# A product-based recommender network on one NeuronCore: all whole row chunks moved by SyncE through a DRAM passage

## What is computed

```python
embed = tables[jnp.arange(26)[None, :], sparse_inputs]      # 2048 x 26 x 32, float32
p   = jnp.einsum('bfe,bge->bfg', embed, embed)
l_z = jnp.einsum('bfe,feh->bh', embed, w_z)                 # h = 256
l_p = jnp.einsum('bfg,fgh->bh', p, w_p)
l_1 = relu(concatenate([l_z + l_p + l_b, dense_inputs], axis=-1))   # dense: 13
h   = relu(l_1 @ W1 + b1)                                   # 128
out = sigmoid(h @ Wf + bf)                                  # 2048 x 1
```

## Time and profile before

| | |
|---|---|
| time, median of 3 runs | 599.81 us (599.52 to 599.99) |
| span of the profiled execution, first to last instruction | 548.8 us |
| POOL busy | 409.0 us (75%), 430 instructions |
| DVE busy | 417.5 us (76%), 250 instructions |
| ACT busy | 139.7 us (25%), 333 instructions |
| PE busy | 131.1 us (24%), 204 passes |
| mean granted TensorE clock | 0.683 of full speed |
| DMA: indirect gathers | 13312 packets, 6.84 MB |
| DMA: issued by SyncE | 6318 packets, 2.63 MB |

### The profile page before, as it was taken

How to read it: one execution, slowest core, us unless ns; L and a number is a source line. 1 busy time by engine, 2 the same in 40 slices (tenths; PEclk the granted TensorE clock), 3 DMA queues, 4 the chain that set the end, 5 groups by cost and what they waited for, 6 DMA issues and landing times.

```text
span 548.8 us, 1701 instructions
## 1 busy us (share of the span) xinstructions
PE 131.1 (24%) x204; PEld 48.0 (9%) x204; DVE 417.5 (76%) x250; ACT 139.7 (25%) x333; POOL 409.0 (75%) x430
## 2 busy tenths in 40 slices
PE   0000000415334100060465100051433600005067
PEld 0000000201111000020121000020110100002023
DVE  4204199998992369998996419999899547999995
ACT  0000004404551021704452010340455110250323
POOL 6777777777777777777777777777777777777792
PEclk9999999976567555585666655567665555558569
DMA  6222323122122222222112222222112222312220
GB/s 148 21 14 13 13 13 14 13 13 14 14 13 13 13 13 14 13 14 13 13 14 14 13 13 13 13 14 13 14 13 13 14 14 13 14 13 13 13 46 2
DMA packets 19640, 9.56 MB, mean 17 GB/s; under 512 B 9888, under 2 KB 19629, under 8 KB 19629
## 3 DMA queue, kind: packets, MB, share of 16 engines
q0 software_dynamic: 13312, 6.84, 22.4%
q1 hardware_dynamic: 6318, 2.63, 2.1%
HBM read 8.85 MB, written 0.01 MB: 16 GB/s over the span
## 4 chain that ended last, share of the span: by engine, by line
POOL 69%; issue 23%; DVE 6%; DMA 1%; PE 1%; ACT 0%; ACTq 0%; POOLq 0%; DVEq 0%
POOL rows L286 66%; DVE pairs L368 3%; DVE prod L348 2%; POOL prod L302 2%; POOL prod L313 1%; DMA rows<-in_L_rec_tables,which 1%; PE ps_h L643 0%; DMA raw<-in_r_sparse_inputs 0%; DVE pair_rows L404 0%; PE ps_h L680 0%; ACT scores L551 0%; PE ps_copy L692 0%; ACT hidden L537 0%; ACTq L120 0%; DVE pairs_T L395 0%
## 5 line engine op out<-in xcount | busy, mean ns | idle before, releaser
L286 POOL DMA_INDIRECT rows<-in_L_rec_tables,which x416 | 393.5, 946 | 128.4 <-issue 125.8
L348 DVE TENSOR_TENSOR prod<-ps_copy,rows 128x1664 f32<-128x1664 f32 (+12 forms) x103 | 194.2, 1910 | 16.8 <-ACT ps_copy L471 16.8
L368 DVE TENSOR_REDUCE pairs<-prod 128x76 f32<-128x2432 f32 (+13 forms) x73 | 195.3, 2680 | 0.0
L626 PE MATMUL ps_h<-field_rows,wz 128*128 128x512 f32 x96 | 59.4, 784 | 290.3 <-ACT field_rows L482 285.4
L379 DVE STREAM_TRANSPOSE rows_T<-rows 128x512 f32<-128x512 f32 (+1 forms) x28 | 18.6, 663 | 98.1 <-DMA rows<-in_L_rec_tables,which 90.7
L471 ACT COPY ps_copy<-rows 128x128 f32<-128x128 f32 (+2 forms) x63 | 21.2, 336 | 273.3 <-DMA rows<-in_L_rec_tables,which 273.0
L643 PE MATMUL ps_h<-pair_rows,w_pair 96*128 96x512 f32 (+2 forms) x64 | 50.2, 943 | 100.3 <-ACT pair_rows L505 84.4
L482 ACT COPY field_rows<-rows_T 32x512 f32<-32x512 f32 (+1 forms) x112 | 58.7, 524 | 34.9 <-DVE rows_T L379 33.4
L626 PEld LDWEIGHTS ps_h<-field_rows,wz 128*128 128x128 f32 x96 | 23.8, 258 | 328.0 <-issue 292.1
L505 ACT COPY pair_rows<-pairs_T 32x256 f32<-32x256 f32 (+1 forms) x96 | 33.5, 349 | 63.1 <-DVE pairs_T L391 61.9
L643 PEld LDWEIGHTS ps_h<-pair_rows,w_pair 96*128 96x128 f32 (+2 forms) x64 | 17.7, 296 | 130.4 <-ACT pair_rows L505 71.9
(11 more groups left out here) (37 smaller groups left out, 31.7 us busy)
## 6 DMA issues: line engine op xcount, KB each, us to landing
rows<-in_L_rec_tables,which POOLq DMA_INDIRECT x416, 3.4
wz<-in_L_rec_w_z SPq DMA_DIRECT2D x1, 768.0 KB, 5.8
field_rows<-rows_T SPq DMA_DIRECT2D x16, 32.0 KB, 1.9
w_pair<-in_w_low SPq DMA_DIRECT2D x1, 288.0 KB, 5.4
w_back<-in_w_high SPq DMA_DIRECT2D x1, 288.0 KB, 5.7
raw<-in_r_sparse_inputs SPq DMA_DIRECT2D x1, 156.0 KB, 2.2
w<-in_L_rec_W SPq DMA_DIRECT2D x1, 128.0 KB
dense_in<-in_r_dense_inputs SPq DMA_DIRECT2D x1, 104.0 KB, 3.2
```

The lines of the kernel that those rows point to most:

```text
L286: nc.gpsimd.indirect_dma_start(rows[:, r % 2, f, k, :], None, table_rows, bass.IndirectOffsetOnAxis(ap=which[:, t, f:f + 1], axis=0),).the ...
L348: ins = nc.vector.tensor_tensor(products(r, s)[:, 0:tiles, at:at + g + 1, :], own.broadcast_to([P, tiles, g + 1, E]), rows[:, r % 2, 0:g + ...
L368: nc.vector.tensor_reduce(pairs[:, 0:tiles, first:end], products(r, s)[:, 0:tiles, :, :], AX.X, ALU.add)\
L626: ins = nc.tensor.matmul(ps_h0[:, h, :], wz[:, j, h * P:(h + 1) * P], field_rows[:, j, :, :, :].rearrange("p q t b -> p (q t b)"), start=( ...
```

## The change

ACT's `lay_rows` is gone, for all groups, and so is SyncE's move L248. SyncE now moves all six whole chunks of every group, each by itself. For a chunk it waits until DVE has turned it, issues four transfers (one for each partition quarter q, 64 KB each) from `rows_T` into a new DRAM tensor `passage`, which has a place for each chunk, waits for their landing (`passed[j]`), and issues one transfer of 256 KB from `passage` into `field_rows`, with 2048 contiguous bytes for each of the 128 partitions (`rows_in[j]`). Over four groups that is 24 x 5 = 120 transfers. DVE's turn of a chunk waits for `passed[j]` of the group before in place of `rows_laid`. PE waits for each chunk by itself; its order changes too: `sum_lz` for chunks 0 to 4 now stands ahead of the product blocks 0 and 1, and only chunk 5 behind `sum_dense`.

```diff
--- before.py
+++ after.py
@@ -62,11 +62,6 @@
     EARLY = NP - (P - LATE)
     TAIL = BLOCKS
 
-    MOVES = [(0, 4), (4, MOVED), (MOVED, CH)]
-    NM = len(MOVES)
-
-    SP_MOVE = 1
-
     PAIR_MOVES = [(0, 2), (2, 3), (TAIL, TAIL + 1)]
     NPM = len(PAIR_MOVES)
     COPIES = 4
@@ -95,9 +90,6 @@
 
     def unit_of(r, f):
         return next(u for u, (first, end) in enumerate(UNITS[r]) if first <= f < end)
-
-    def move_of(j):
-        return next(m for m, (first, end) in enumerate(MOVES) if first <= j < end)
 
     def pair_move_of(c):
         return next(m for m, (first, end) in enumerate(PAIR_MOVES) if first <= c < end)
@@ -155,6 +147,8 @@
         hidden0 = sb("hidden0", [P, HALVES, BANK])
         hidden1 = sb("hidden1", [H1, BANK])
         scores = sb("scores", [1, BATCH])
+
+        passage = nc.dram_tensor("passage", (MOVED, PER, E, QUADS, K * Q), F32).ap()
 
         ps_copy = ps("ps_copy", [P, COPIES, PER, K, E])
         ps_h0 = ps("ps_h0", [P, HALVES, BANK])
@@ -184,7 +178,8 @@
         pool_multiplied = sem("pool_multiplied")
         pool_added = sem("pool_added")
         pool_summed = sem("pool_summed")
-        rows_moved = sem("rows_moved")
+        passed = [sem(f"passed_{j}") for j in range(MOVED)]
+        rows_in = [sem(f"rows_in_{j}") for j in range(MOVED)]
         last_rows_moved = sem("last_rows_moved")
         rows_turned = sem("rows_turned")
         rows_laid = sem("rows_laid")
@@ -239,16 +234,22 @@
             sp.dma_start(bf_one[:, :], bf.rearrange("(p o) -> p o", o=1)).then_inc(mlp_in, DMA)
 
 
+            for r in range(ROUNDS):
+                for j in range(MOVED):
+                    sp.wait_ge(rows_turned, CH * r + j + 1)
+                    if r:
+                        sp.wait_ge(rows_in[j], DMA * r)
+                    for q in range(QUADS):
+                        sp.dma_start(passage[j, :, :, q, :].rearrange("u e x -> e u x"),
+                                     rows_T[Q * q:Q * (q + 1), j, :, :, :].rearrange("p u k b -> p u (k b)"))\
+                            .then_inc(passed[j], DMA)
+                    if r:
+                        sp.wait_ge(lz_summed, MOVED * (r - 1) + j + 1)
+                    sp.wait_ge(passed[j], DMA * QUADS * (r + 1))
+                    sp.dma_start(field_rows[:, j, :, :, :].rearrange("p q k b -> p (q k b)"),
+                                 passage[j, :, :, :, :].rearrange("u e q x -> (u e) (q x)")).then_inc(rows_in[j], DMA)
+
             r = ROUNDS - 1
-            first, end = MOVES[SP_MOVE]
-            sp.wait_ge(rows_turned, CH * r + end)
-            sp.wait_ge(lz_summed, MOVED * (r - 1) + end)
-            for q in range(QUADS):
-                for u in range(PER):
-                    sp.dma_start(field_rows[Q * u:Q * (u + 1), first:end, q, :, :].rearrange("p c k b -> p c (k b)"),
-                                 rows_T[Q * q:Q * (q + 1), first:end, u, :, :].rearrange("p c k b -> p c (k b)"))\
-                        .then_inc(rows_moved, DMA)
-
             sp.wait_ge(rows_turned, CH * (r + 1))
             sp.wait_ge(lp_summed, (TAIL + 1) * r)
             for q in range(QUADS // 2):
@@ -375,7 +376,10 @@
                     first, end = UNITS[r][u]
                     dve.wait_ge(landed[r][u], DMA * K * (end - first))
                 if r:
-                    dve.wait_ge(rows_laid, NM * (r - 1) + move_of(j) + 1)
+                    if j < MOVED:
+                        dve.wait_ge(passed[j], DMA * QUADS * r)
+                    else:
+                        dve.wait_ge(rows_laid, r)
                 nc.vector.transpose(rows_T[:, j, 0:n, :, :].rearrange("p f k b -> p (f k b)"),
                                     rows[:, r % 2, PER * j:PER * j + n, :, :].rearrange("p f k e -> p (f k e)"))\
                     .then_inc(rows_turned, 1)
@@ -471,19 +475,6 @@
                 nc.scalar.copy(ps_copy[:, (NU * r + u) % COPIES, 0:end - first, :, :],
                                rows[:, r % 2, first:end, :, :]).then_inc(copied, 1)
 
-            def lay_rows(r, m, q):
-
-                first, end = MOVES[m]
-                if q == 0:
-                    act.wait_ge(rows_turned, CH * r + end)
-                    if r:
-                        act.wait_ge(lz_summed, MOVED * (r - 1) + end)
-                for u in range(PER):
-                    ins = nc.scalar.copy(field_rows[Q * u:Q * (u + 1), first:end, q, :, :],
-                                         rows_T[Q * q:Q * (q + 1), first:end, u, :, :])
-                if q == QUADS - 1:
-                    ins.then_inc(rows_laid, 1)
-
             def lay_last_rows(r):
                 act.wait_ge(rows_turned, CH * (r + 1))
                 if r:
@@ -561,16 +552,8 @@
                         make_hidden1(r - 1)
                     if r and first == 8:
                         make_scores(r - 1)
-                    if first in (14, 16, 17, 18):
-                        lay_rows(r, 0, (14, 16, 17, 18).index(first))
                     if 20 <= first < 23:
                         lay_pairs(r, 0, first - 20)
-                    if first == 23:
-                        lay_rows(r, SP_MOVE, 0)
-                    if first == 24:
-                        lay_rows(r, SP_MOVE, 1)
-                for q in range(2, QUADS):
-                    lay_rows(r, SP_MOVE, q)
                 for u in range(PLACES):
                     lay_pairs(r, 1, u)
                 lay_last_rows(r)
@@ -587,8 +570,6 @@
                     make_hidden1(r - 1)
                 if first == 8:
                     make_scores(r - 1)
-                if 15 <= first < 19:
-                    lay_rows(r, 0, first - 15)
                 if 22 <= first < 24:
                     lay_pairs(r, 0, first - 22)
                 if first == 24:
@@ -618,10 +599,7 @@
                     pe.wait_ge(wz_in, DMA * 2)
                 if r and j == 0:
                     pe.wait_ge(hidden0_made, HALVES * r)
-                if r == ROUNDS - 1 and move_of(j) == SP_MOVE:
-                    pe.wait_ge(rows_moved, DMA * QUADS * PER)
-                else:
-                    pe.wait_ge(rows_laid, NM * r + move_of(j) + 1)
+                pe.wait_ge(rows_in[j], DMA * (r + 1))
                 for h in range(HALVES):
                     ins = nc.tensor.matmul(ps_h0[:, h, :], wz[:, j, h * P:(h + 1) * P],
                                            field_rows[:, j, :, :, :].rearrange("p q t b -> p (q t b)"),
@@ -634,7 +612,7 @@
                     pe.wait_ge(w_pair_made, 1)
                 pe.wait_ge(pairs_laid, NPM * r + pair_move_of(c) + 1)
                 if c == TAIL:
-                    pe.wait_ge(rows_laid, NM * (r + 1) - (1 if r == ROUNDS - 1 else 0))
+                    pe.wait_ge(rows_laid, r + 1)
                     if r == ROUNDS - 1:
                         pe.wait_ge(last_rows_moved, DMA * QUADS // 2 * LAST)
                     pe.wait_ge(tail_turned, r + 1)
@@ -699,13 +677,12 @@
                 nc.tensor.matmul(ps_end[0:1, :], wf[:, :], hidden1[:, :], start=True, stop=True).then_inc(logit_made, 1)
 
             for r in range(ROUNDS):
-                for j in range(*MOVES[0]):
+                for j in range(MOVED - 1):
                     sum_lz(r, j)
                 for c in range(*PAIR_MOVES[0]):
                     sum_lp(r, c)
                 sum_dense(r)
-                for j in range(*MOVES[1]):
-                    sum_lz(r, j)
+                sum_lz(r, MOVED - 1)
                 for c in range(*PAIR_MOVES[1]):
                     sum_lp(r, c)
                 sum_lp(r, TAIL)
```

## The result

| kernel | runs | median us (lowest to highest) | ratio to before, 95% interval |
|---|---|---|---|
| before | 6 | 599.88 (599.47 to 600.10) | |
| changed | 6 | 597.94 (597.42 to 598.52) | 0.9972 [0.9961, 0.9983] |

1.9 us faster, outside the predicted range and on its other side. The profiled execution of the changed kernel took 598.52 us. From its page: span, shares of the chain, the gathers.

The account below looks back on a forecast made before the run. POOL's gathers were taken to bound the kernel, DVE its end. Terms 0 (ACT, SP, DVE waits) + 0 (POOL's pitch) + 1.8 (clock) + 0.3 (landing) = +2.1 on 599.8 gave 601.9 us, range 599.4 to 602.8.

Parts of the forecast that it names:

- the one that tied the profile to the time: Whole kernel: the 51.0 us between span 548.8 and median 599.81 left as they are, 2.1 added to 599.8.
- if the gap between median and span moves away from 51 us: Whole kernel, new profile: one of the signs named in advance that would show the prediction wrong.
- L248 at 0: End of last group: removing 16 transfers with 10.36 us of issue gains nothing, as TAIL waited 0.50 us for DVE.
- The slow TAIL at +1.8: Last TAIL block: four passes at granted clock 0.50, 3.75 us against 1.95, delay hidden0: +1.8 us, ends 0 and +2.5.
- Sign and size: Whole kernel: slower by 2.1 us, 0.35%; chance of slower 0.52.
- POOL's pitch 0: POOL's 416 gathers: 0.946 us each and their gaps unchanged, taken as 0; upper bound 0.35 us.
- Chunk 5's data: Last group: through DRAM with 2.5 us for the write and 3.0 for the read, there at 529.1 us.
- The idle time ahead of block 2 and the clock: PE, last group: idle 3 to 5 us, block 2 slow at 3.78 us, idle 1.6 us, then TAIL at clock 0.50.
- rival 1's second way: PE's end: block 2's 3.8 us alone lift the clock by TAIL, time the same, 600.1; rival's chance 0.39 over both ways.
- Gathers' landing +0.3: Fields 16 and 17, last group: chunk 3's passage traffic delays gather landings by 0.3 us, ends -0.45 and +2.2.
- The faster rival: Fields 16 and 17 land better and the clock stays up: 599.4, gain at most 0.45 us; within that bound chance 0.01.
- the part outside the span: Time beyond the profiled span: its shrinking, or DVE's or POOL's work shrinking, needed for a gain over 1.2 us.

Follow-up runs that it names:

- b0: The kernel before, unchanged, profiled again and timed beside itself: 598.5 against 598.4 us, ratio 1.000.
- e6: The changed kernel plus eight dead matmuls ahead of the last TAIL: 598.35 us against 599.61 for the kernel before, ratio 0.9976.
- a1: The changed kernel, run again on the chip where the kernel before takes 550.85 us: 553.29 us, ratio 1.0042.
- e5 again: Kernel before, only the last group's chunks 4 and 5 through DRAM, PE's new order there, ACT's copies kept; second run: 552.87 against 550.85 us, ratio 1.0034.
- e12: The changed kernel plus eleven dead transfers issued behind chunk 6's four: 553.99 us against 550.85 for the kernel before, ratio 1.0046.
- e3: The changed kernel with the last group's chunk 4 summed behind the dense part again: 597.86 us against 599.61 for the kernel before, ratio 0.9970.
- e9: The kernel before with the last group's L248 replaced by 16 ACT copies: 601.69 us against 598.38 for the kernel before, ratio 1.0050.

## Why the prediction was wrong

**The step that failed is the one that tied the profile to the time**: "the median of the runs shown is 599.81, 51.0 us above that span; what those 51.0 us hold is not in the trace, and I leave it as it is". They were not something outside the span. In b0 and in the changed kernel's own profile a span lies 2.1 us under its execution's time; the 51 us were about 2 us and another kind of execution, in which many gathers take longer from gather 172 on and gaps of issue open on the other engines (96.3 us ahead of DVE's products, by b0's page). The text named "if the gap between median and span moves away from 51 us" as a sign of being wrong; it was 2.1.

**The two terms that this turned over.** *L248 at 0, as TAIL "waited 0.50 us for DVE, not for them"*: in the shown execution there were 10.36 us of issue and it was so. In the timed one they are 19.35 us, followed by 5.07 for L256, which TAIL needs. This term, put at nothing, is worth -1.2 us by the table of N (26.93 less 25.77), and -1.5 to -1.9 by the times; that it acts through TAIL's wait for L256 is argued, not shown, in b0. *The slow TAIL at +1.8*: it came, 3.75 us long, and costs 0, since 4.2 us of another wait follow it (e6: 1.88 us for TAIL, same hidden0).

**The rest, on the ground where it was worked out (a1).**
- *Sign and size*: predicted +2.1, measured +2.4 (1.4 to 3.3).
- *POOL's pitch 0*: 945 ns and 126.5 us of gaps against 946 and 125.8.
- *Chunk 5's data*: forecast 529.1, 7.4 us after the turn's end; measured 529.92, 7.9 after it. An issue is 0.44 us where 0.6 was taken. The slowest of chunk 5's writes of 64 KB landed after 3.8 us (2.5 taken), its read of 256 KB after 2.6 (3.0 taken): two misses that partly cancel. The median landings over the span are 2.7 and 3.8 us. The Trainium skill ("DMA: Bandwidth & Descriptors", section on the anatomy of one DMA) put them at 2.15 and 2.6 and the data at 528.3: for chunk 5 too short on the write and right on the read, and 1.6 us too early in all, by a1's trace. That section's figures are for transfers that GpSimd issues, and these are SyncE's. A hop that is too slow is not what costs the time here: PE waited 3.22 us for chunk 5's data and had them at 529.92, where the direct transfers of before held it for 4.92 us, until 533.47. They come earlier, and by my reading that is what tears the burst ahead of TAIL apart; no run on that chip puts it together again.
- *The idle time ahead of block 2 and the clock*: forecast 3 to 5 us, found 2.31. Block 2 took 2.22 us, mostly at the higher clock (granted 0.91 from 536 to 538 us), where 3.78 was forecast; the passes ahead of it were chunk 5's, 3.78 us at a granted 0.50. The clock rose one block earlier than in rival 1's second way, and that didn't help: 3.22 us of idle time follow (1.6 forecast), and TAIL takes 3.44 us: the rows of the stretches give a granted clock of 0.50 from 541 to 543 us and 0.64 from 543 to 545. DVE's half of hidden0 starts at 544.93, forecast "about 545.0"; ACT's half of hidden1 at 546.48, 1.77 us later than in the earlier trace rows: 1.49 of it TAIL's longer run (3.44 less 1.95), 0.27 its later start. The second layer was fast here, as taken, but partly slow in e5 again and e12, whose TAIL took 3.75 us. Whether the whole cost would go with a faster clock was not shown there: e6 and e3 never ran on that chip.
- *Gathers' landing +0.3*: DVE starts field 16's product at 482.46 after a wait of 1.45 us, against 481.75 and 0.16, finds field 17 ready, and ends the TAIL transposes at 541.31 against 541.03: +0.3.

**Rivals and range.** The faster rival was bounded at 0.45 us; "the part outside the span" was named as a way to more, and "faster" got 0.08 in all. The range covered errors within the shown execution only. That the size comes out on the chip of the shown profile is to the credit of the working there; that it wasn't the kind of execution that is timed could have been asked before. An unexplained 51 us, 9% of the time, should have made both the range and the chance of a gain far larger.

## What to carry to other kernels

Set the span of a profile beside the execution's own time before any row is used: here 2 us apart is the rule, and 51 us meant that the profile showed an execution in which other waits came last. Then price the removed work for both: a burst of 16 transfers cost nothing where one was issued every 0.65 us, and 1.2 to 1.9 us where it was one every 1.2. A change of a few tenths of a per cent at the end of a kernel can have both signs on different chips; say on which it was measured.

## What was not expected of the hardware

- The same program took 598.4 to 599.6 us on three chips and 550.85 on a fourth, steadily (its executions there lie between 550.40 and 551.37). The difference grows from about gather 172 on (mean gather over the whole kernel 1.023 us in b0 against 0.945 in a1).
- In the stretched part it isn't the long instructions that suffer: DVE's product of 3072 columns takes 3.32 us in both, but in places a copy of 0.30 us comes only every 1.4 us (e9, from 568.8 us on), and a transfer is issued only every 1.2 us in place of 0.65 (L248 in b0). Short bursts escape it: four transfers of chunk 6 take 2.48 us in the changed kernel at 566.39 as in a1, and 5.07 in b0 at 577.90. What is shared there, and why 20 transfers and not 13 show, stays open.
